# The opening of a three-layer CIN tower, rearranged: ids, weights, factor loads and dense features

## What is computed

```python
h = e
for W, b in ((W0, b0), (W1, b1), (W2, b2)):          # 128 columns each
    z = einsum('bfd,bgd->bfgd', e, h)                 # every pair of fields
    cur = relu(einsum('bfgd,fgl->bld', z, W) + b)
    h, direct = cur[:, :64], cur[:, 64:]              # last layer: all 128 are direct
rec = concat(directs).sum(-1)                         # (1024, 256)
x = concat([rec, dense_ctx])                          # 256 + 16 columns
y = relu(relu(x @ W_top1 + b_top1) @ W_top2 + b_top2) @ W_top3
```

## Time and profile before

| | us |
|---|---|
| median of 3 runs | 1365.14 (1364.8 to 1367.58) |
| the profiled execution | 1367.65 |
| its span, first to last instruction | 1366.0 |
| TensorE busy | 1247.5 (91%) |
| VectorE busy | 1044.1 (76%) |
| GpSimd busy | 998.2 (73%) |
| ScalarE busy | 727.2 (53%) |

### The profile page before, as it was taken

One profiled execution on the slowest core, in us unless ns is written; L12 is line 12 of the kernel. 1 busy time (PEld: TensorE's weight loads), 2 busy tenths in 40 slices (PEclk: granted clock), 3 DMA queues, 4 the chain that ended last, 5 costly groups with the idle time before them and its releaser, 6 DMA issues.

```text
span 1366.0 us, 15702 instructions
## 1 busy us (share of the span) xinstructions
PE 1247.5 (91%) x3980; PEld 729.5 (53%) x3980; DVE 1044.1 (76%) x944; ACT 727.2 (53%) x943; POOL 998.2 (73%) x607
## 2 busy tenths in 40 slices
PE   0025999999999999999999999999999999999999
PEld 0012565555555555655555555556555555655545
DVE  0115878899888888888898788888888988889731
ACT  2102556656655565556566555655565666556432
POOL 6770368898888888888888888888888865556511
PEclk9996999999999999999999999999999999999999
DMA  8097256667766656666776656666576766655000
GB/s 172 11 182 148 46 121 125 131 136 141 140 130 124 122 116 122 123 122 131 136 140 140 137 119 119 120 123 128 115 129 137 140 138 138 132 121 141 1 0 1
DMA packets 101052, 160.50 MB, mean 117 GB/s; under 512 B 17322, under 2 KB 29467, under 8 KB 100845
## 3 DMA queue, kind: packets, MB, share of 16 engines
q1 hardware_dynamic: 90715, 156.66, 56.4%
q0 software_dynamic: 10240, 2.74, 2.0%
HBM read 155.47 MB, written 6.19 MB: 118 GB/s over the span
## 4 chain that ended last, share of the span: by engine, by line
PE 51%; POOL 22%; issue 20%; another core or an unknown queue 3%; DVE 2%; ACT 2%; DMA 1%; POOLq 0%; DVEq 0%; ACTq 0%
PE curM L757 25%; POOL zl L261 12%; POOL emb L250 9%; PE curM L774 7%; PE curM L766 6%; PE curM L767 6%; PE curY L757 4%; DVE z L474 2%; PE h L842 2%; ACT h L624 1%; PE xk L842 1%; PE curY L842 1%; PE curY L767 0%; PE curY L766 0%
## 5 line engine op out<-in xcount | busy, mean ns | idle before, releaser
L261 POOL TENSOR_TENSOR zl<-z,zh 128x1024 fp32r<-128x1024 f32 (+1 forms) x281 | 673.6, 2403 | 277.1 <-ACT zh L607 267.3
L474 DVE TENSOR_TENSOR z<-xr,h 128x1024 f32<-128x1024 f32 x576 | 668.7, 1211 | 23.4 <-PE curM L757 13.9
L757 PE MATMUL curM<-z,wf 128*128 128x512 f32 (+2 forms) x1290 | 585.0, 602 | 17.6 <-issue 17.6
L607 ACT ACTIVATE zh<-z 128x1024 fp32r<-128x1024 f32 (+1 forms) x352 | 367.9, 1054 | 295.1 <-DVE z L474 252.7
L250 POOL DMA_INDIRECT emb<-in_tbl_dram,idx x312 | 319.1, 1023 | 70.2 <-issue 59.5
L766 PE MATMUL curM<-zh,wl 128*128 128x512 f32 (+1 forms) x642 | 345.5, 538 | 11.9 <-ACT zh L607 9.9
L757 PEld LDWEIGHTS curM<-z,wf 128*128 128x128 f32 (+2 forms) x1290 | 227.8, 189 | 230.5 <-issue 208.8
L525 DVE TENSOR_TENSOR zl<-z,zh 128x1024 fp32r<-128x1024 f32 (+1 forms) x71 | 136.7, 1925 | 175.7 <-ACT zh L607 175.7
L767 PE MATMUL curM<-zh,wh 128*128 128x512 f32 (+1 forms) x642 | 252.2, 393 | 0.0
L774 PE MATMUL curM<-zl,wh 128*128 128x512 f32 (+1 forms) x642 | 205.1, 401 | 5.6 <-POOL zl L261 4.5
L766 PEld LDWEIGHTS curM<-zh,wl 128*128 128x128 f32 (+1 forms) x642 | 121.7, 189 | 86.4 <-issue 50.5
(11 more groups left out here) (94 smaller groups left out, 372.1 us busy)
## 6 DMA issues: line engine op xcount, KB each, us to landing
xr<-xT SPq DMA_DIRECT2D x384, 192.0 KB
xs<-xT SPq DMA_DIRECT2D x96, 546.0 KB
xq<-xT SPq DMA_DIRECT2D x64, 256.0 KB
emb<-in_tbl_dram,idx POOLq DMA_INDIRECT x312
xT<-xc SPq DMA_DIRECT2D x32, 78.0 KB
xr<-in_L_rec_W_dram SPq DMA_DIRECT2D x16, 144.0 KB
xT<-xc SPq DMA_DIRECT2D x32, 40.0 KB
xs<-in_W_top_dram SPq DMA_DIRECT2D x2, 512.0 KB, 6.5
```

The source lines that it names most:

```text
L261: nc.gpsimd.tensor_tensor(zl[0:n, SNUM[r, u] % NL, :], z[0:n, z_slot(r, u), :], zh[0:n, SNUM[r, u] % NH, :], ALU.subtract).then_inc(lo_poo ...
L474: return nc.vector.tensor_tensor(z[:, slot, :].rearrange("p (a n) -> p a n", a=2), x, h, ALU.mult)
L607: nc.scalar.activation(zh[0:n, SNUM[r, u] % NH, :], z[0:n, z_slot(r, u), :], ACT.Copy).then_inc(hi_ready, 1)
L757: mm = nc.tensor.matmul(cur[:, :], wf[rows, full_at(u), a, :], z[rows, z_slot(r, u), a * N:(a + 1) * N], start=start and i == 0, stop=stop ...
```

## The change

The ids of the first two blocks are loaded by SP, ahead of everything else on its queue. GpSimd makes the identity first and then issues its gathers; the first 32 fields of block 0 count on a semaphore of their own, and ScalarE copies the gathered rows in two parts, the first after those 32.

Weights are handled in runs of units: equally spaced units of one kind are one instruction. ScalarE only rounds (4 instructions), VectorE makes the full copies (10 instructions, three of which are the sums of `W0` written straight to `wf`) and the low parts (4).

The factor `xs` has four semaphores and is loaded in four pieces, one for each layer 0 unit: 3 + 3 + 3 + 2 transfers in place of 3. Each product waits for its own piece, and each piece is issued after the product that last used its place. In the opening the order becomes: write 0, write 1, (all weights done), `xs` of step 0, write 2, `xs` of step 1, `xr` and `xq` of step 0, `xs` of step 2, `xr` and `xq` of step 1. The wait for the weights now stands behind the first two writes.

The dense features are loaded in the opening, repeated seven times by ScalarE to 112 columns, turned by eight transposes (into `curY` and `curM[1]`) and copied to `dT` with two instructions. The 16 rows of `W_top1` that belong to them are loaded in four blocks at partitions 0, 32, 64 and 96 (`wC`). At the end the 16-row products of two groups are issued one after the other, ahead of the 128-row products of both.

```diff
+            sp.dma_start(idx[0][:, :], ids[0:P, :]).then_inc(first_idx_loaded[0], 16)
+            sp.dma_start(idx[1][:, :], ids[P:2 * P, :]).then_inc(first_idx_loaded[1], 16)
...
-            load_ids(0, 0)
-            load_ids(1, 1)
             nc.gpsimd.memset(ident[:], 1.0).then_inc(ident_zeroed, 1)
-            pool.wait_ge(idx_loaded[0], 16)
-            for f in range(F):
-                gather(f, 0)
             pool.wait_ge(ident_zeroed, 1)
             nc.gpsimd.affine_select(out=ident[:], in_=ident[:], compare_op=ALU.is_equal, fill=0.0, base=0,
                                     pattern=[[-1, P]], channel_multiplier=1).then_inc(ident_ready, 1)
-            pool.wait_ge(idx_loaded[1], 16)
+            pool.wait_ge(first_idx_loaded[0], 16)
             for f in range(F):
-                gather(f, 1)
+                gather(f, 0, gathered_first if f < FIRST_FIELDS else gathered[0])
+            pool.wait_ge(first_idx_loaded[1], 16)
+            for f in range(F):
+                gather(f, 1, gathered[1])
...
-            def load_xs(t):
-                for k in range(K):
-                    nt = T0 if k < 2 else T0 - 1
-                    src = bass.AP(xT.tensor, (t * XR + k) * N, [[N, F], [K * N, T0], [1, N]])
-                    sp.dma_start(xs[k * F:(k + 1) * F, :].rearrange("p (t c) -> p t c", c=N), src).then_inc(xs_loaded, 16)
+            def load_xs(t, p):
+
+                for k in range(K if p < 3 else 2):
+                    nt = 2 if p < 3 else 1
+                    src = bass.AP(xT.tensor, (t * XR + k + 2 * p * K) * N, [[N, F], [K * N, nt], [1, N]])
+                    sp.dma_start(xs[k * F:(k + 1) * F, 2 * p * N:(2 * p + nt) * N].rearrange("p (t c) -> p t c", c=N),
+                                 src).then_inc(xs_loaded[p], 16)
...
-            sp.wait_ge(w_hi, 2 * UNITS - 1)
-            sp.wait_ge(w_lo, 2 * (UNITS - nf))
             sp.wait_ge(xc_copied, 1)
             write_x(0, 0)
             sp.wait_ge(xc_copied, 2)
             write_x(1, 1)
+            sp.wait_ge(w_hi, HI_OPS)
+            sp.wait_ge(w_lo, LO_OPS)
+            sp.wait_ge(w_full, FULL_OPS)
             sp.wait_ge(xT_written[0], 32)
-            load_xs(0)
+            for p in range(4):
+                load_xs(0, p)
             sp.wait_ge(xc_copied, 3)
             write_x(2, 0)
-            load_xq(0, 0)
+            sp.wait_ge(xT_written[1], 32)
+            for p in range(4):
+                sp.wait_ge(z_ready, NUM[-3, C_END + p] + 1)
+                load_xs(1, p)
             for k in range(3):
                 load_xr(0, 0, k)
-            sp.wait_ge(xT_written[1], 32)
-            sp.wait_ge(z_ready, NUM[-3, UNITS - 1] + 1)
-            load_xs(1)
-            load_xq(1, 1)
+            load_xq(0, 0)
+            sp.wait_ge(xT_written[0], 64)
+            for p in range(4):
+                sp.wait_ge(z_ready, NUM[-2, C_END + p] + 1)
+                load_xs(2, p)
             for k in range(3):
                 load_xr(1, 1, k)
-            sp.wait_ge(xT_written[0], 64)
-            sp.wait_ge(z_ready, NUM[-2, UNITS - 1] + 1)
-            load_xs(2)
+            load_xq(1, 1)
...
+            for w, loaded in enumerate((w1_loaded, w2_loaded)):
+                act.wait_ge(loaded, 16 * 10)
+                for run in SPLIT_RUNS[w]:
+                    n, at = len(run), split_at(run[0])
+                    nc.scalar.activation(wh[:, at:at + n, :, :], staged_run(w, run), ACT.Copy).then_inc(w_hi, 1)
...
+            act.wait_ge(dense_loaded, 16 * 5)
+            nc.scalar.activation(dn7, dn.unsqueeze(2).to_broadcast([P, NB, 7, DN]), ACT.Copy).then_inc(dense_spread, 1)
+            act.wait_ge(dense_turned, 1)
+            nc.scalar.activation(dT[:, 0:N], curY[0:7 * DN, :], ACT.Copy).then_inc(dense_copied, 1)
+            nc.scalar.activation(dT[:, N:B], curM[1][0:7 * DN, :], ACT.Copy).then_inc(dense_copied, 1)
...
             for i in range(14):
                 cur, cols, n = top_bank(i), *top_cols(i)
-                need = {8: 5, 9: 6, 10: 8, 11: 8, 12: 10, 13: 12}.get(i, i - 3)
+                if i < 8 and i % 2 == 0:
+
+                    if i >= 4:
+                        pe.wait_ge(top_read, i - 2)
+                    for g in (i, i + 1):
+                        m = slice(g % 4 * Q, g % 4 * Q + DN)
+                        nc.tensor.matmul(top_bank(g)[:, 0:n], wC[m, :], dT[m, cols], start=True, stop=False)
+                need = {8: 5, 9: 6, 10: 8, 11: 8, 12: 10, 13: 12}.get(i, 0)
```

More of the change, by code:

```diff
@@ L87, in rows0, with runs @@
     return R0 if t < T0 - 1 else R0_LAST
+def runs(units):
+    found = []
+    for u in units:
+        if found and (len(found[-1]) == 1 or u - found[-1][-1] == found[-1][-1] - found[-1][-2]):
+            found[-1].append(u)
+        else:
+            found.append([u])
+    return found
+PAIRED = [u for u in range(UNITS) if u not in (A_END - 1, A_END) and u < C_END]
+SPLIT_RUNS = [runs([u for u in PAIRED if (u < A_END) == (w == 0) and KINDS[u] != "F"]) for w in range(2)]
+FULL_RUNS = [runs([u for u in PAIRED if (u < A_END) == (w == 0) and KINDS[u] == "F"]) for w in range(2)]
+FIRST_FIELDS = 32
 def cin_tower(nc, dense, ids, tables, w_top1, b_top1, w_top2, b_top2, w_top3, w0, w1, w2, b0, b1, b2, out):
@@ L247, in load_ids, with gather @@
                 pool.dma_start(idx[slot][:, :], ids[bass.ds(b * P, P), :]).then_inc(idx_loaded[slot], 16)
-            def gather(f, slot):
+            def gather(f, slot, done):
                 nc.gpsimd.indirect_dma_start(
@@ L252, in gather @@
                     in_offset=bass.IndirectOffsetOnAxis(ap=idx[slot][:, f:f + 1].bitcast(U32), axis=0),
-                ).then_inc(gathered[slot], 16)
+                ).then_inc(done, 16)
             def subtract(r, u, j):
@@ L382, in _ @@
                 sp.dma_start(stage0r[k * F:(k + 1) * F, t:nt, :], src).then_inc(w0_loaded, 16)
+            sp.dma_start(dn, dense.rearrange("(j p) c -> p j c", p=P)).then_inc(dense_loaded, 16)
+            for m in range(M1 // P):
+                sp.dma_start(wC[m * Q:m * Q + DN, :], w_top1[2 * P:2 * P + DN, m * P:(m + 1) * P]).then_inc(dense_loaded, 16)
             with nc.allow_non_contiguous_dma(reason="a few small columns"):
@@ L801, in _ @@
             pe.wait_ge(ident_ready, 1)
+            pe.wait_ge(dense_spread, 1)
+            for c in range(NB):
+                to = curY if c < DQ else curM[1]
+                mm = nc.tensor.transpose(to[0:7 * DN, c % DQ * P:(c % DQ + 1) * P],
+                                         dn7[:, c, :, :].rearrange("p g c -> p (g c)"), ident[:, :])
+            mm.then_inc(dense_turned, 1)
             pe.wait_ge(emb_copied, 1)
@@ L841, in _ @@
                 for q, (w, v) in enumerate(parts):
-                    mm = nc.tensor.matmul(cur[0:w.shape[1], 0:n], w, v, start=q == 0, stop=q == len(parts) - 1)
+                    mm = nc.tensor.matmul(cur[0:w.shape[1], 0:n], w, v, start=i >= 8 and q == 0, stop=q == len(parts) - 1)
                 mm.then_inc(top_done, 1)
@@ L849, in _ @@
             for m in range(4):
+                rows = slice(m * Q, m * Q + DN)
+                nc.tensor.matmul(end_bank(m)[:, 0:P], wC[rows, :], dT[rows, CC], start=True, stop=False)
+            for m in range(4):
                 mc = slice(m * P, (m + 1) * P)
-                nc.tensor.matmul(end_bank(m)[:, 0:P], wAB[:, 0, mc], zs[:, 0, CC], start=True, stop=False)
-                nc.tensor.matmul(end_bank(m)[:, 0:P], wC[:, mc], zC[1][:, N - P:N], start=False, stop=False)
+                nc.tensor.matmul(end_bank(m)[:, 0:P], wAB[:, 0, mc], zs[:, 0, CC], start=False, stop=False)
             pe.wait_ge(allB, NB)
```

166 lines of the change are left out of this document (90 added, 76 removed).

## The result

The changed kernel takes 1349.75 us (1348.38 to 1350.93, 4 runs) against 1365.45 for the kernel before: a ratio of 0.9882, interval 0.9865 to 0.9899, 15.7 us less. I had forecast 1358, some 7 us less, within 1325 to 1370. The sign was right and the range held, but it was wide: the measured time lies under the 1353 to 1363 of the likeliest case, and the size was not right. The profiled execution has a span of 1346.6, against 1366.0. That is 19.4 us: the profiled execution of the changed kernel was its fastest, and that of the kernel before (1367.65) slower than all its timed runs, so parts read from the two traces add up to 3.7 us more than the medians differ by.

What follows compares the result with a forecast made beforehand. TensorE, busy 91% of the span, was taken as the bound, leaving only the opening and last 65 us; opening 3.0 plus end 4.0 made 7.0, from 1367.65 to 1360.6 profiled, 1358 for the median, range 1325 to 1370.

Steps and rivals of the forecast that it cites:

- the likeliest case: Whole kernel: ScalarE's late reading stays and ends with the gathers; opening 3.0, end 4.0, 1353 to 1363 us; chance 0.40.
- the hold: Opening: ScalarE's layer 0 reading waits for TensorE's count, due at 91.76, and goes 25.12 us later; likeliest to stay.
- rival A: Opening: ScalarE gets TensorE's count in time, layer 1 starts 33 or 19 us earlier, 1328 or 1342 us; chance 0.33.
- B: Opening: ScalarE's late reading stays at 116.88 whatever gathers do; only the end gains, 1361 or 1363 us; chance 0.12.
- order, pieces: Opening: block 1's factor precedes xr of block 0, products start piece by piece; buys nothing if ScalarE's reading stays late.
- the split copy: Opening: ScalarE copies 32 of 39 embedding fields during the gathers, so the copy ends sooner; gains 0.9 us.
- ids and identity: Opening: ids from SP 2.7 us (0.5 to 3.7), identity moved before gather 1 0.3; gathers end 3.0 us earlier.
- Weights in runs: Opening: fewer weight instructions on ScalarE and VectorE cost nothing, gathers cover them; without that cover up to 18 us.
- The end: Last stage: transposes gone, fewer row switches, last columns reordered; sum 4.0 us, bounds 2.1 and 4.0 + 3.4.
- Running at once: Top stage: paired 16-row products overlap in different row groups; upper bound 3.4 us, not counted in the 4.0 taken.
- the switches between 16 and 128 rows: Top stage: each switch costs 0.40 in a group, half of them go, 8 x 0.2 = 1.6 us.
- The very end: Last 128 columns: the same order of 16-row products may give 0.3 us, an estimate.

Runs made afterwards that it cites:

- 4: Changed kernel with the opening loads in their former order, still in pieces; 1348.68 us, ratio 0.9897.
- 5: Changed kernel with the former order of opening loads and the factor loaded whole in three transfers; 1348.8 us, ratio 0.9893.
- 16: Changed kernel with the embedding of block 0 copied in one part, behind the 39th gather; 1349.3 us, ratio 0.9896.
- number 10: Changed kernel with the first two loads of ids put back on GpSimd's queue; 1352.86 us, ratio 0.9919.
- 2: Kernel before with only the dense features turned up front (identity ahead of the gathers) and the new top stage; 1365.94 us, ratio 1.0016.
- number 12: Changed kernel with the weights converted tile by tile again; 1354.3 us, ratio 0.9935.
- number 11: Kernel before with only the weights converted in runs of tiles; 1360.97 us (10 runs), ratio 0.9975.
- number 3: Changed kernel with the 16 rows of W_top1 at partitions 0 to 15 for all four column blocks; 1351.7 us, ratio 0.991.
- 13: Changed kernel, block 1's gathers resumed once block 0's rows landed (2 us idle), 28 at once, 11 spread over round 0; 1336.53 us, ratio 0.9808.
- number 6: Changed kernel with a gap: block 1's gathers wait for round -3's products, then 28 at once, 11 spread over round 0; 1316.01 us, ratio 0.9651.
- number 7: Kernel before with only a gap in the gathers, ended by round -3's last product (about 29 us); 1355.37 us, ratio 0.9929.

## Why the prediction was right in sign and wrong in size

**The opening.** *Right:* the hold stays, rivals A and B did not come about, and as long as it lasts order, pieces and the split copy buy nothing (numbers 4, 5, 16). *Right in mechanism:* the end of the hold follows the stream of gathers. Ids on SP's queue start it 3.85 us earlier (6.92 to 3.07; the sum had 2.7, and 3.7 as its most) and are worth 3.1 us at the reading and in the medians and 3.8 in the span (number 10). The whole term of 3.0 for ids and identity stands.

*The step that failed* is "Weights in runs. ... I cost it at nothing: the gathers cover it." I had looked at when the last subtraction starts, and not at what 69 small counted instructions do to what is counted behind them. (In the trace the runs are 5 on ScalarE and 12 and 5 on VectorE, not 4, 10 and 4.) The hold ends some time behind the stream, and this time depends on the weights:

| kernel | weights | first gather | last gather | reading | from last | from first |
|---|---|---|---|---|---|---|
| before | by tile | 6.92 | 104.16 | 116.88 | 12.7 | 110.0 |
| new end alone (2) | by tile | 6.90 | 104.03 | 116.99 | 13.0 | 110.1 |
| by tile again (12) | by tile | 2.96 | 100.23 | 112.82 | 12.6 | 109.9 |
| runs alone (11) | in runs | 6.89 | 104.11 | 114.57 | 10.5 | 107.7 |
| changed | in runs | 3.07 | 102.55 | 109.61 | 7.1 | 106.5 |
| one row group (3) | in runs | 3.04 | 100.86 | 108.00 | 7.1 | 105.0 |
| old order (4) | in runs | 2.96 | 100.85 | 109.02 | 8.2 | 106.1 |
| old order, whole (5) | in runs | 3.04 | 102.09 | 110.17 | 8.1 | 107.1 |
| ids on GpSimd (10) | in runs | 6.84 | 105.48 | 112.70 | 7.2 | 105.9 |
| one copy (16) | in runs | 3.05 | 101.25 | 109.66 | 8.4 | 106.6 |
| short gap (13) | in runs | 2.89 | 88.87 | 96.89 | 8.0 | (28 gathers) |

Taken from the first gather, the two kinds fall apart cleanly: 109.9 to 110.1 us with weights by tile, 105.0 to 107.7 in runs. The last gather is a poorer mark, because the stream itself is longer in the changed kernel: four of its gathers (19.50, 20.99, 27.84 and 76.12) take 1.19 to 2.41 us in place of 0.94. So of the 7.26 us, 3.1 are the ids (number 10), and the weights are 2.3 taken alone (number 11) or 3.2 at the reading when taken back (112.82 against 109.61, number 12). Some 1 to 2 us go to neither; the five kernels alike in both (changed, 3, 4, 5, 16) are themselves up to 2.2 apart. By the medians the weights gave 2.3, and taken back they cost 4.6, and 6.1 by the spans (1352.7 against 1346.6). The larger figures take in that they keep the dense features from doing harm: in numbers 2 and 12 the dense turn stood behind the small weight copies, and each copy of the embedding came late. In the changed kernel ScalarE spreads the dense features at 32.03 and TensorE turns them by 35.

**The end.** By size this term was missed by more than the weights: the sum had 4.0 and bounds up to 7.4; the traces show 9.2 (6.93 and 2.27). The transposes and copies gave what was said: from the last product before them to the first behind them it takes 1.80 us (1289.02 to 1290.82) in place of 4.00 (1299.22 to 1303.22), 2.2 against the 2.12 forecast. Running at once, the term that I had left to the upper bound (3.4) and put at nothing in the sum, gave 3.0 (number 3). The Trainium skill ("TensorE: Matmul & The Clock Gate", Part 3, The mechanism) says that products in different row groups overlap. The trace agrees, with two records at 1295.51 and 1295.52. What is left of 6.93 is 6.93 - 2.2 - 3.0 = 1.7 for the switches between 16 and 128 rows, forecast 1.6; it is a remainder, and no run shows it by itself.

The very end was mis-sized most by its ratio: 0.3 forecast, 2.27 measured. Two rows cut it, the first products that need the last sums `zs`, before and after:

```profile
1358.67 1.18 PE L856 MATMUL h<-zs,xs 128*128 128x128 f32 x4
```

```profile
1340.70 0.71 PE L926 MATMUL h<-zs,xs 128*128 128x128 f32 x4 [0.70 <-DVE zs L589]
```

From ScalarE's last reading to these it takes 3.02 us before (1355.65 to 1358.67) and 2.18 now (1338.52 to 1340.70), 0.84 less. The four groups themselves got shorter by more (3.2 to 1.3 us), but TensorE now waits for VectorE's sums. From there to the end of the span the instructions are the same in both, and they take 7.33 us before and 5.90 now, 1.43 less. These are rows of the kernel before, and then of the changed one, in that last part (length, busy us by engine, clock, DMA share, GB/s):

```profile
1357.00:1360.00 3.00, 3.00 (x15) 2.51 (x15) 0.74 (x2) 0.48 (x2) 0.00 (x0) 0.79 0.00 0
1360.00:1363.00 3.00, 3.00 (x20) 3.00 (x18) 0.00 (x0) 1.35 (x4) 0.00 (x0) 0.64 0.00 0
```

```profile
1341.00:1344.00 3.00, 3.00 (x26) 2.70 (x24) 0.00 (x0) 1.67 (x6) 0.00 (x0) 1.00 0.00 0
```

TensorE was granted 0.79 and 0.64 of full speed there, a mix of its two levels of 2.4 and 1.2 GHz, and 1.00 in the changed kernel. While the four groups ran (1355.0 to 1358.6) it was 1.00 before too. Ahead of the fall the groups had alternated between 16 and 128 rows without a pause; in the changed kernel the 16-row products stand together, and a wait for VectorE follows them. Which of these differences kept the clock up wasn't tried.

**The middle.** "TensorE is the bound, so nothing" holds for the 8 more transfers a round: most rounds take 37.3 to 37.4 us in both, and the longest 38.4 before and 38.0 after.

**Where the rest of the gain went.** What rival A promised, 33 us, is there, but the change alone can't collect it. With the gap the first layer 1 product starts at 81.88; the forecast for A was 91. And the parts that the prediction dismissed for want of an effect (order, pieces) are worth 11.3 and 15 us there. The hold had made a kernel with better loads look the same as one without.

**What stays open.** Which part of the chip serves the counts at so slow a pace isn't shown. The runs show only one condition: a stream of gathers that has not paused, near 52 to 65 us, for some 7 to 12 us. Whether its early start, ahead of the weights, is another was not tried. That the small weight instructions act by the counts they send, and not by their number or their time on ScalarE, is argued from their spacing (1.4 us apart from 30.96 on in the kernel before, each taking 0.31); numbers 11 and 12 change all three at once. Nor is it shown whether the hold is there in an execution of which nothing is recorded.

## What to carry to other kernels

When an engine waits tens of microseconds on a count that is long due, look for a stream of gathers that has run without a pause, and break it for some 10 us where the handshakes of the opening are: one wait gave over 31 us here, twice what the whole change gave, and 8.6 in the kernel before, where late data was the next limit. Cost small counted instructions also by what waits behind them, not only by their time under a cover. And judge a reordering of loads only after such a hold is gone, since it hides what they are worth. Where products of few rows stand between products of 128 rows, put them together and into different row groups: the top stage gained 4.7 us by that (3.0 + 1.7) and the very end 0.8.

## What the runs showed of the hardware

- While the hold lasts, a transfer's issue on SP takes 1.34 us (14.70/11), with the DMA engines at 0.45 of their time, and 0.41 (4.53/11) right behind it. So the slow issue of the hold is not the fullness of the DMA engines. Beside full engines an issue took 0.50 us in number 6 (6.04/12, xr at 71.49) and 1.17 in number 7 (14.03/12 at 87.61).
- A count between two engines came 25.1 us (before) and 25.7 us (changed kernel) late while 78 gathers ran in a row, 1.25 us apart. A pause of 12 us in the gathers ended that, one of 7 us nearly did, one of 2 us did not. With 28 gathers in a row from 70.42 on, beside full DMA engines, ScalarE's reading was not held.
- Two 16-row products in different row groups (four records) take the time of one: 1.06 us from 1290.82 to 1291.88, against 1.05 for the one product (two records) of the kernel before, from here to 1306.15:

```profile
1305.10 1.12 PE L842 MATMUL h<-xc,xs 16*128 16x512 f32 x2
```
